# Output projection and experts' input in one stage of eight units, and the first attention loads issued during the projection

## The reference, cut to what matters

```
h   = layernorm(x) * (1 + scale_a) + shift_a
x   = x + gate_a * (attention(h) @ Wo + bo)       # the output projection
z   = layernorm(x) * (1 + scale_m) + shift_m      # the experts' input
      # layer 1 only: x goes on as x + gate_m*z, and the experts get layernorm(z) * g + b
lg  = z @ gate_w (+ bias)                         # router: 8 logits a token
x   = x + gate_m * sum over the top 2 experts of p_e * expert_e(z)
```

## Time and profile before

| | us |
|---|---|
| median of 3 runs | 2500.89 (2485.25 to 2501.75) |
| the profiled execution | 2496.8 |
| its span on the core | 2494.9 |
| layer 0: `project`, `attend` | 30 to 211.4, 211.4 to 544.3 |
| layer 0: `out_project`, `moe_input` | 544.3 to 590.5, 590.5 to 675 |
| layer 1: `project`, `attend` | 1225.6 to 1380.5, 1380.5 to 1944.1 |
| layer 1: `out_project`, `moe_input` | 1944.1 to 1990.3, 1990.3 to 2116 |

### The profile page before, as it was taken

One profiled execution on the slowest core, in us unless ns is written; L12 is line 12 of the kernel. 1 busy time (PEld: TensorE's weight loads), 2 busy tenths in 40 slices (PEclk: granted clock), 3 DMA queues, 4 the chain that ended last, 5 costly groups with the idle time before them and its releaser, 6 DMA issues. The chain is left out here.

```text
span 2494.9 us, 46728 instructions
## 1 busy us (share of the span) xinstructions
PE 1932.4 (77%) x15652; PEld 1349.0 (54%) x15652; DVE 1669.4 (67%) x3311; ACT 1089.1 (44%) x2227; POOL 820.3 (33%) x692
## 2 busy tenths in 40 slices
PE   5994888976638999998199599999998724289991
PEld 2773666755537899987054233333333523177771
DVE  3664566646778666665589587888774577765555
ACT  2772444443526333332166066666566344232222
POOL 1454333430234333332067211111111033356650
PEclk8996999987559999999599599999999855599996
DMA  4337988822336211111535824444420101242226
GB/s 142 127 138 159 183 161 169 171 67 86 129 108 191 91 52 48 48 52 35 201 138 180 147 45 69 69 69 69 69 36 2 30 32 64 94 125 84 82 77 223
DMA packets 176821, 253.47 MB, mean 102 GB/s; under 512 B 29380, under 2 KB 118500, under 8 KB 174564
## 3 DMA queue, kind: packets, MB, share of 16 engines
q1 hardware_dynamic: 157124, 205.50, 33.0%
q0 software_dynamic: 14976, 40.91, 5.3%
q10 hardware_dynamic: 4512, 4.24, 0.5%
HBM read 170.59 MB, written 79.21 MB: 100 GB/s over the span
## 5 line engine op out<-in xcount | busy, mean ns | idle before, releaser
L848 DVE TENSOR_REDUCE a_mx<-a_pmx 128x1 f32<-128x512 f32 (+5 forms) x928 | 506.0, 589 | 184.9 <-PE a_pmx L714 80.9
L912 ACT ACTIVATE a_probs<-a_pst 128x512 f32<-128x512 f32 (+2 forms) x864 | 426.0, 552 | 359.4 <-PE a_pst L732 194.9
L709 PE MATMUL a_pmx<-a_Ks,a_Qs 96*128 96x192 bf16 (+4 forms) x1280 | 344.9, 309 | 64.0 <-DMA a_V<-v_d 62.7
L1841 PE MATMUL m_ph<-m_zh,m_w 128*128 128x256 f16 x2808 | 327.9, 277 | 37.5 <-DVE m_w L1216 18.3
L1841 PEld LDWEIGHTS m_ph<-m_zh,m_w 128*128 x2808 | 274.0, 99 | 86.0 <-issue 50.1
L1857 PE MATMUL m_py<-m_w,m_zh 128*128 x2808 | 319.2, 273 | 0.6 <-DVE m_free L1907 0.4
L732 PE MATMUL a_pst<-a_Qs,a_Ks 99*128 99x192 bf16 (+5 forms) x1344 | 306.8, 291 | 9.3 <-ACT a_probs L912 6.1
L1857 PEld LDWEIGHTS m_py<-m_w,m_zh 128*128 128x128 f16 x2808 | 271.0, 98 | 32.0 <-issue 1.3
L1887 ACT ACTIVATE x_res<-m_ph,m_b,m_s 128x256 f32<-128x256 f32 x312 | 159.2, 561 | 247.3 <-PE m_ph L1841 239.3
L709 PEld LDWEIGHTS a_pmx<-a_Ks,a_Qs 96*128 96x128 bf16 x1280 | 125.1, 100 | 238.2 <-DVE a_mx L848 128.1
L1794 POOL DMA_INDIRECT m_zh<-z_d,m_src x156 | 171.2, 1098 | 225.5 <-PE m_pt L1824 182.9
(11 more groups left out here) (281 smaller groups left out, 3260.7 us busy)
## 6 DMA issues: line engine op xcount, KB each, us to landing
parts_d<-p_part SPq DMA_DIRECT2D x64, 384.0 KB, 3.2
a_Qs<-parts_d SPq DMA_DIRECT2D x192, 128.0 KB, 4.5
a_Ks<-parts_d SPq DMA_DIRECT2D x192, 128.0 KB, 7.2
v_d<-p_vt SPq DMA_DIRECT2D x16, 1024.0 KB, 4.4
a_V<-v_d SPq DMA_DIRECT2D x32, 512.0 KB, 9.1
m_got<-y_d SPq DMA_DIRECT2D x32, 512.0 KB, 6.6
a_wst<-L_w1T SPq DMA_DIRECT2D x16, 512.0 KB, 6.4
a_wst<-L_w2T SPq DMA_DIRECT2D x16, 512.0 KB, 4.9
```

Source lines behind the costliest of these rows:

```text
L709: mm = nc.tensor.matmul(pmx[:, buf, o:o + cols], Qs[par][0:KROWS, h, i * P:(i + 1) * P], Ks[par][0:KROWS, h, k0:k1], start=True, stop=not ...
L848: nc.vector.tensor_reduce(mx[:, part, hs[0]:hs[0] + len(hs), i], src, AX.X, ALU.max).then_inc(m_done, 1)
L912: nc.scalar.activation(probs[:, (hg * NV + v) % 2, hs[0]:hs[0] + len(hs), q0:q1], src, ACT.Exp, scale=HD ** -0.5).then_inc(exp_done, 1)
L1841: mm = nc.tensor.matmul(ph[:, (G * par + g) % 4, q * ROWS:(q + 1) * ROWS], self.w1[:, bass.ds(e, 1), c, wp, m * P:(m + 1) * P].rearrange(" ...
```

## The change

- `out_project` and `moe_input` become one block, `post`, unrolled, with 8 units of four tiles (two pairs). In slot k TensorE multiplies the pairs 2k and 2k+1 by the output weights, transposes the pairs 2k+2 and 2k+3, and then does the logits of unit k-1 (k-2 in layer 1: `FINAL`). VectorE adds both pairs to x, takes the statistics of unit k, scales unit k-1, and so on.
- The gate is multiplied into the output weights (`wog`, GpSimd, once a batch), and gate times bias is added to x by GpSimd during the attention (`add_bias`). Of VectorE's three operations a pair one is left (`add_x`), and the transposes read `attn` without ScalarE's copy.
- `wo`, `bo` and `gate` are loaded when the attention starts. The rows and small weights of the experts' input are loaded at the start of `post`, needed in its slots 0 and 1. x and z are stored once a unit.
- The attention's sets 0, 1 and 2 are loaded during the last pass of `project`, in its slots 1, 3 and 5 (`EARLY`), behind that slot's store.
- In layer 0's attention SP issues the experts' weights ahead of the maxima instead of behind them, and `dve_turn` moves from odd steps to the even steps after.

```diff
+            EARLY = (1, 3, 5)
...
+                        if isinstance(b, int) and b == B - 1 and k in EARLY:
+                            if k == EARLY[0]:
+                                for half in range(2):
+                                    sp.wait_ge(v_out[half], 16)
+                                for i in range(4):
+                                    sp.wait_ge(part_out[i], 16 * 2)
+                            self.load_set(sp, layer, EARLY.index(k), 0, EARLY.index(k))
...
+            turn_at = {("st", 2 * e + 2, a): (e, a // 6) for e in range(EXPERTS - 1) for a in (3, 6)}
+            turn_at.update({("st", STEPS - 1, NE - 4): (EXPERTS - 1, 0), ("st", STEPS - 1, NE - 2): (EXPERTS - 1, 1)})
...
-                    if NORM and s % 2 and kind == "st" and a in (3, 6):
-                        dve_turn(dve, s // 2, a // 6)
+                    if NORM and (kind, s, a) in turn_at:
+                        dve_turn(dve, *turn_at[kind, s, a])
...
+                    def add_bias(s):
+                        b = s // SETS
+                        if s % SETS == 0:
...
+                            nc.gpsimd.tensor_tensor(bog[:, :], bo[:, :], self.gate[:, b, :], ALU.mult).then_inc(bog_ready, 1)
...
+                        nc.gpsimd.tensor_tensor(xs, xs, bog[:, :].unsqueeze(1).broadcast_to([P, 2, D]), ALU.add).then_inc(x_biased, 1)
...
+                            add_bias(2 * e)
+                            add_bias(2 * e + 1)
...
+                            if n == len(diagonal) // 2 - 1:
+                                add_bias(j)
...
-                    for hg in range(SETS - 1):
-                        if hg > 0:
-                            sp.wait_ge(kq_in[hg - 1], 16 * loads)
-                        load(sp, hg, 0, hg)
+                    late()
...
-                            send_max(sp, (hg + 1) % SETS, s + 1)
                             if NORM:
                                 load_weights(sp, 2 * b + hg // 2, hg % 2, s)
+                            send_max(sp, (hg + 1) % SETS, s + 1)
```

The core of `post`, engine by engine (ScalarE's, TensorE's and VectorE's loops, without layer 0's scales and layer 1's second normalisation):

```diff
+                    for k in range(LASTS):
+                        if has(k + 1):
+                            turned(2 * k + 2)
+                            turned(2 * k + 3)
+                        for i in range(NORMS):
+                            if has(n := k - i):
+                                norm(i, n)
...
+                        if has(n := k - FINAL):
+                            act.wait_ge(z_ready[NORMS - 1], n + 1)
...
+                            nc.scalar.activation(zh[:, n % 2, :, 0, :], zs[:, NORMS - 1, n % 2, :, :], ACT.Copy).then_inc(hi_done, 1)
+                            for t in range(HT):
+                                act.wait_ge(tr_done, HT * n + t + 1)
+                                nc.scalar.activation(zT[:, t % 2, :, :], ptr[:, t % 2, 0:D].rearrange("p (c n) -> p c n", c=DC), ACT.Copy).then_inc(zT_ready, 1)
...
+                    for k in range(LASTS):
+                        if has(k):
+                            for u in (2 * k, 2 * k + 1):
+                                project(u)
+                                if u + 2 < PAIRS:
+                                    turn(u + 2)
...
+                        if has(n := k - FINAL):
+                            h = n % 2
+                            pe.wait_ge(z_ready[NORMS - 1], n + 1)
...
+                    for k in range(LASTS):
+                        if has(k):
+                            add_x(2 * k)
+                            add_x(2 * k + 1)
+                            dve.wait_ge(x_added, 2 * k + 2)
+                            moments(0, k)
...
+                        if has(k - 1):
+                            scale(0, k - 1)
+                        if has(k):
+                            inverse(0, k)
```

More of the change, by code:

```diff
@@ L38 @@
 HALF = 512
+SETS = 4
+LOADS = 2 * SLOTS + 1
+SLOT_Q, SLOT_K = (0, 0, 0, 1, 1, 2), (0, 1, 2, 0, 1, 0)
 HT = HALF // P
@@ L612, in key_blocks, with load_set @@
         return out
+    def load_set(self, sp, layer, par, b, hg):
+        pd = self.parts_d[layer]
+        row = lambda base: bass.ds(hg * (HG * HD) + base, HG * HD)
+        for dst, base, slots in ((self.Qs[par], 0, SLOT_Q), (self.Ks[par], D, SLOT_K)):
+            for s, part in enumerate(slots):
+                src = pd[part, row(base), bass.ds(b * L, L)].rearrange("(g e) n -> e g n", e=HD)
+                sp.dma_start(dst[s * HD:(s + 1) * HD, :, :], src).then_inc(self.kq_in[par], 16)
+        vsrc = self.v_d[layer][bass.ds(b * L, L), bass.ds(hg * (HG * 2 * HD), HG * 2 * HD)].rearrange("(t p) n -> p t n", p=P)
+        sp.dma_start(self.V4[par][:, :, :, :].rearrange("p t h e -> p t (h e)"), vsrc).then_inc(self.kq_in[par], 16)
     def attend(self, layer):
@@ L671, in attend @@
             mask = self.causal if layer else self.window
[L672 to L681, removed]
-                        sp.dma_start(dst[s * HD:(s + 1) * HD, :, :], src).then_inc(kq_in[par], 16)
-                vsrc = self.v_d[layer][bass.ds(b * L, L), bass.ds(hg * (HG * 2 * HD), HG * 2 * HD)].rearrange("(t p) n -> p t n", p=P)
-                sp.dma_start(V4[par][:, :, :, :].rearrange("p t h e -> p t (h e)"), vsrc).then_inc(kq_in[par], 16)
+            loads = LOADS
+            load = lambda sp, par, b, hg: self.load_set(sp, layer, par, b, hg)
             def load_weights(sp, e, second, s):
@@ new lines, in post @@
+            KINDS = (2, 3, 1) if twice else (2, 3)
+            NORMS = FINAL = 2 if twice else 1
+            rows = sb("rows", [P, len(KINDS), B, D])
+            lnr = sb("lnr", [P, 2, D]) if twice else None
+            wog = sb("wog", [P, 2, DC, D])
+            ones = sb("gones", [P, P])
+            gg = sb("gg", [P, EXPERTS])
+            gsq = sb("gsq", [P, DC, EXPERTS])
+            eps = sb("eps", [P, 1])
+            as4 = lambda a, shape, **k: a[:, :, :, :].rearrange("p t h e -> p (t h e)").rearrange(shape, **k)
@@ new lines, in post @@
+            aT = as4(self.V4[2], "p (u t c n) -> p u t c n", u=2, t=2, c=DC)
+            stats = sb("stats", [P, NORMS, HT, nc.vector.BN_STATS_DIM])
+            mv = sb("mv", [P, NORMS, 2, HT, 2])
+            sd = sb("sd", [P, NORMS, 2, HT])
+            rstd = sb("rstd", [P, NORMS, 2, HT])
+            shift = sb("shift", [P, NORMS, 2, HT])
+            zs = sb("zs", [P, NORMS, 2, HT, D])
+            gh = [as4(self.V4[i], "p (t d) -> p t d", d=D) for i in range(2)]
+            zT = sb("zT", [P, 2, DC, P])
@@ L1143, in _, with add_x, moments @@
-                    run(dve, slot)
+                    def add_x(u):
+                        xu = self.x[:, 2 * u:2 * u + 2, :]
+                        dve.wait_ge(y_done, u + 1)
+                        nc.vector.tensor_tensor(xu, xu, py[:, u % 2, :].rearrange("p (t n) -> p t n", t=2), ALU.add).then_inc(x_added, 1)
+                    def moments(i, n):
+                        h = n % 2
+                        for t in range(HT):
+                            src = self.x[:, HT * n + t, :] if i == 0 else zs[:, 0, h, t, :]
+                            nc.vector.bn_stats(stats[:, i, t, :], src).then_inc(stats_ready[i], 1)
+                        dve.wait_ge(stats_ready[i], HT * n + HT)
+                        for t in range(HT):
+                            a = nc.vector.bn_aggr(mv[:, i, h, t, :], stats[:, i, t, :])
+                        a.then_inc(mv_ready[i], 1)
```

640 lines of the change are left out of this document (274 added, 366 removed).

## The result

The changed kernel takes 2612.64 us (median of 4 runs, 2605.37 to 2614.5) against 2497.99 us before: a ratio of 1.0463, 95% interval 1.0419 to 1.0507. The forecast was 2543 us, with a range of 2490 to 2575. The direction was right and the size was not: +115 us in place of +46, 2.5 times as much. The profiled execution has a span of 2603.5 us, 108.6 more than before.

A forecast was written before the change was run, and what follows sets the result against it. In the stages to be fused no engine was busy all the time; waits and seams counted. Terms +23 + 14 + 0 + 9 + 0 = +46 us on 2496.8 gave 2543 us, range 2490 to 2575.

The forecast's parts named there:

- Part 1: Fused stage `post`: each slot's operations on three engines form one row of waits; +23 us in layer 0, +14 in layer 1.
- the middle between the ends: Layer 1's fused stage: slot of 24.8 us, taken between 22 at full clock and 27.6 at half.
- the half-clock end of 27.6: Layer 1's fused stage: slot length in us if TensorE's clock stays at half.
- Part 2: GpSimd's bias additions and gate products: small, taken as 0, ends 0 and +8 us over both layers.
- Part 3: Set loads in the last projection passes: stores held, projections end 23 and 27 us later; net 0 and +9 us.
- The seams: Projection to attention: later projection ends against saved load waits; 0 us in layer 0, +9 in layer 1.
- Part 4: Layer 0's attention: VectorE's waits go, up to -20 us, but maxima follow weights; taken as 0, ends -20 and +10.
- up to 7 us: Layer 0's attention: delay of the maxima behind 1 MB of weights on the queue, at a set's rate.
- (a): Projection: early loads cost it nothing, stores land in time; seams -23 and -17 us, 2494 us; chance 0.14.
- (b): Fused stage: TensorE keeps its full clock; -10 us in all, 2487 us; chance 0.12.
- (d): Fused stage: the loop isn't closed and units overlap as in `moe_input`; 2461 us; chance 0.05.
- (c): Fused stage: TensorE stays at half clock all through; +88 us in all, 2585 us; chance 0.12.

The follow-up runs named there:

- e4: Changed kernel with TensorE's output products one slot earlier in `post`, ahead of the logits there: 2483.59 us, 0.9922 of the kernel before.
- e8: Changed kernel with maxima first, products a slot earlier, and layer 0's bias additions ahead of the first expert's squares: 2431.2 us, 0.9723 of the kernel before.
- e11: e3 with GpSimd's bias additions in layer 0's attention ahead of the first expert's squares: 2574.7 us.
- e6: Changed kernel with maxima first, products a slot earlier, and all three sets loaded at the attention's start again: 2435.55 us, 0.9746 of the kernel before.
- e7: Changed kernel with maxima first, products a slot earlier, and only one set loaded during the projection: 2421.5 us, 0.9685 of the kernel before.
- e2: Changed kernel with layer 0's attention turns back in odd steps, weights still ahead of the maxima: 2596.33 us, 1.0382 of the kernel before.
- e3: Changed kernel with both layer 0 attention edits undone, maxima first and turns in odd steps: 2575.52 us, 1.0283 of the kernel before.
- e9: e2 with one more unused 1 MB copy ahead of the weights in each of layer 0's 16 attention steps: 2615.09 us, 1.046 of the kernel before.

## Why the prediction was wrong

**Part 1, the closed loop: right in mechanism, short in size.** The slots are the row of waits that the prediction wrote down, and e4 shows it: taking one link out of the loop gives 129 us. The sizes were 18.9 against 18 in layer 0 and 27.4 against 24.8 in layer 1, so +30 and +24 in place of +23 and +14. The reading of the clock, half in the first products of a burst and full in the second, stands in the rows (3.52 and 1.89 us). In layer 1 the middle between the ends was too low; the slot is near the half-clock end of 27.6, at a clock of 0.61. The fused stage by itself was not the error: in e4 it is 34 and 36 us shorter than the two blocks before the change.

**Part 2, bias and gate: right.** e8 and e11 move them for 2.6 and 0.8 us.

**Part 3, loads in the projection: right in mechanism, a little too dear.** The stores do stand behind the loads, and ScalarE waited 20.3 and 25.8 us for them, against 23 and 27; the projections end 17.7 and 19.5 us later. The seams came to -3 and +2 where I had 0 and +9. e6 confirms that the whole is worth nothing, and e7 that one set of three was the one worth taking.

**Part 4, layer 0's attention: the step that failed.** "But the maxima now follow 1 MB of weights on the queue ... I take 0 here, ends -20 and +10." The attention took 57 us more. Both halves of the sentence were in front of me and I let them cancel, with an upper end below the price that I had just named (up to 7 us in each of 16 steps). Two things were wrong. The first is that I had treated the move of the turn as a gain to be set against the order on SP, where the runs show that each edit removes the same wait of VectorE, so that the second has nothing left to gain and its price is paid in full: 21 us with the turns in odd steps (e2 against e3), 52 with the turns in even ones (the change against e1). The second is that I had a price and looked for no slack to set it against. In an odd step there is none: set, weights and maxima go out back to back, the maxima of the step at 311.97 land at 337.5, and TensorE waits 8.6 us, 5.9 in the mean of the six waits, near the "up to 7 us" of the forecast. That wait makes the even step long, its own maxima are issued 17.9 to 24.1 us into it, and they land 2 to 4 us after their issue with nobody waiting. So the price falls on every second step. What picks the even steps for the wait isn't shown; e2, with the turns in the odd steps, has it there too.

The hold of SP at the weights, which the move of the turn brought in (GpSimd's square waits for the turn, and SP for the square), was my first theory. It is in the trace, 10 us in an even step, but the maxima behind it go out 0.02 us after VectorE has them. And the account isn't complete: with both edits undone (e3) this stretch is still some 23 us longer than before the change. GpSimd's additions are some 3 of these (e11); no run found the rest.

**The rivals.** (a), the loads cost nothing, and (b), the full clock, did not happen; nor did (d). (c), half clock throughout, is near to what layer 1 did. None of them had the attention in it, and the range had its width in the stage that I understood best. Had the attention not changed, the same errors elsewhere would have given +53 us, inside the range.

## What to carry to other kernels

Fusing two pipelined stages pays only if no engine's order joins the end of one unit's chain to the start of the next one's: write down for each engine what stands between unit k's last operation of stage one and unit k-1's last of stage two, and if every link waits for the one before, move the producer a slot ahead (three lines of one loop here, 129 us). A transfer that somebody waits for at once goes ahead of bulk loads on the same queue. Before an issuer's wait is called a cost, look when the data behind it were ready: SP stood 10 us at the weights here and still sent the maxima as soon as VectorE had them. Two edits against the same wait are not two gains, and can be a loss.

## What the runs showed of the hardware

One more megabyte ahead of small transfers on SP's queue lengthened TensorE's wait for them by 3.0 us each time (e9 against e2), not by the 7 us that a set's rate gives; why sets take so much longer for their bytes wasn't tried. And VectorE's operations on the maxima are longer beside GpSimd's. Before the change the last two took 0.21 and 0.28 us (at 334.34 and 334.58, GpSimd idle). In the changed kernel's even step, with GpSimd's addition below them:

```profile
302.08 0.86 DVE L880 CAST a_nmp<-a_nmr 32x128 bf16<-32x128 f32 x1
302.98 2.46 DVE L882 TENSOR_TENSOR a_nmp<-a_nmr,a_nmp 32x128 bf16<-32x128 f32 x1
...
302.95 3.69 POOL L958 TENSOR_TENSOR a_wsq<-a_wsq 128x1024 f32<-128x1024 f32 x2
```

GpSimd had also been squaring from 300.98 to 302.87, so both lie beside its work; the first of them ends at 302.94, just after that square. The Trainium skill ("SBUF — State Buffer", section "Who interferes with whom") has a rule for it, that VectorE and GpSimd take turns at one pair of ports, each for a whole instruction; the operation that read two tiles and took 2.46 us agrees with it. That is some 3 us more until the maxima are ready, and no run told it apart from the rest of the 16 us between the change and e2. In e2's even step, with GpSimd idle from 300.34, the same two operations took 0.21 and 0.28 us.
